# The two rings of matmul outputs in a mixture-of-experts stage, each cut to a depth of one

## The reference, cut to what matters

```python
x = x + _L0_gnn_ref(xn, edge_index, ...) + _L0_mix_ref(xn[None], ...)[0]
x = x + _L0_ffn_ref(_layernorm(x)[None], ...)[0]
# in _L0_ffn_ref:
#   a softmax over the edges that end in a node weighs the rows of its neighbours -> scores
topk_s, topk_i = jax.lax.top_k(scores, 2); w = softmax(topk_s)
for ei in range(4):
    g = jnp.where(topk_i == ei, w, 0.0).sum(-1)
    hh = jax.nn.gelu(x @ W1[ei] + b1[ei])            # 256 -> 512
    out = out + g[..., None] * (hh @ W2[ei] + b2[ei])  # 512 -> 256
```

## Time and profile before

| | us |
|---|---|
| median of 3 runs | 5559.33 |
| the profiled execution, its own time | 5560.58 |
| its span | 5558.8 |
| PE busy | 3511.5 (63%) |
| PE weight loads busy | 2291.2 (41%) |
| DVE busy | 2083.0 (37%) |
| ACT busy | 802.4 (14%) |
| POOL busy | 2839.8 (51%) |
| TensorE clock granted, mean | 0.801 of full |

### The profile page before, as it was taken

The page is one execution under the profiler, slowest core; times in us unless marked ns, Lnnn a source line. Parts: engine busy times, 40 slices in busy tenths (PEclk is TensorE's granted clock), DMA queues, the critical chain, the costliest instruction groups (busy, mean ns, idle before and its releaser), DMA issues. The chain is left out here.

```text
span 5558.8 us, 46231 instructions
## 1 busy us (share of the span) xinstructions
PE 3511.5 (63%) x12937; PEld 2291.2 (41%) x12938; DVE 2083.0 (37%) x4892; ACT 802.4 (14%) x1970; POOL 2839.8 (51%) x2937
## 2 busy tenths in 40 slices
PE   0688888888577767777242766666666666669300
PEld 0455555555455545555121443434343434346200
DVE  5455566565566555444010111112011111103278
ACT  4111111111011111111010101111111111112000
POOL 2666666666666666666657144444445353530420
PEclk6898999899788888888675888788877878789755
DMA  7444444444455555655121111111111111111297
GB/s 254 116 112 111 114 113 113 110 112 111 112 133 148 148 145 149 166 152 151 20 62 19 32 46 35 42 39 43 38 42 46 35 46 36 46 31 63 87 255 257
DMA packets 381413, 540.56 MB, mean 97 GB/s; under 512 B 120315, under 2 KB 297819, under 8 KB 381144
## 3 DMA queue, kind: packets, MB, share of 16 engines
q0 software_dynamic: 119136, 234.44, 19.2%
q1 hardware_dynamic: 243119, 288.12, 16.2%
q10 hardware_dynamic: 19016, 16.48, 0.9%
HBM read 392.03 MB, written 146.74 MB: 97 GB/s over the span
## 5 line engine op out<-in xcount | busy, mean ns | idle before, releaser
L787 POOL DMA_INDIRECT rows<-xn_rows,gsrc x1664 | 1611.5, 968 | 902.0 <-issue 458.8
L1353 POOL DMA_INDIRECT nb<-route_rows,idx x1024 | 1001.5, 978 | 1087.4 <-DVE msg L1428 772.7
L1092 PE MATMUL PS<-rows,oh 128*128 128x257 f32 x3328 | 908.3, 426 | 339.9 <-issue 215.3
L1682 PE MATMUL PS<-arena,hid 128*125 128x256 f32 x3200 | 773.2, 400 | 524.3 <-ACT hid L1643 311.5
L1674 PE MATMUL PS<-x2g,arena 128*128 128x500 f32 x1600 | 759.4, 634 | 314.8 <-issue 154.5
L1682 PEld LDWEIGHTS PS<-arena,hid 128*125 128x125 f32 x3200 | 633.5, 199 | 680.5 <-issue 577.6
L1092 PEld LDWEIGHTS PS<-rows,oh 128*128 128x128 f32 x3328 | 693.4, 214 | 470.9 <-issue 284.3
L1617 DVE TENSOR_TENSOR y_sb<-PS,b_b 125x512 f32<-125x512 f32 x200 | 128.7, 686 | 2010.5 <-PE PS L1682 1466.4
L1674 PEld LDWEIGHTS PS<-x2g,arena 128*128 128x128 f32 x1600 | 321.2, 204 | 732.1 <-issue 540.1
L1643 ACT ACTIVATE hid<-PS,b_sb 128x500 f32<-128x500 f32 x400 | 270.2, 678 | 1551.1 <-PE PS L1674 762.5
L1164 PE MATMUL PS<-own_w,p_t 128*125 128x512 f32 x400 | 228.8, 656 | 77.6 <-ACT s_t L1052 45.4
(11 more groups left out here) (304 smaller groups left out, 3088.6 us busy)
## 6 DMA issues: line engine op xcount, KB each, us to landing
y_rows<-y_sb SPq DMA_DIRECT2D x100, 512.0 KB
arena<-y_rows SPq DMA_DIRECT2D x100, 512.0 KB
rows<-xn_rows,gsrc POOLq DMA_INDIRECT x1664
nb<-route_rows,idx POOLq DMA_INDIRECT x1024
sum_rows<-kept SPq DMA_DIRECT2D x104, 128.5 KB
x_rows<-x SPq DMA_DIRECT2D x100, 128.0 KB
hid<-x_rows SPq DMA_DIRECT2D x100, 128.0 KB
m_in<-sum_rows SPq DMA_DIRECT2D x100, 125.5 KB
```

The lines of the kernel that those rows point to most:

```text
L787: pool.indirect_dma_start(out=rows[w][h][:, q, 0:D], out_offset=None, in_=xn_rows, in_offset=bass.IndirectOffsetOnAxis(ap=gsrc[:, s * HU + ...
L1092: last = mm(SUM[:, 0:D + 1], oh[w][h][:, q, :], rows[w][h][:, q, :], start=h == 0 and q == 0, stop=h == 1 and q == HU - 1)
L1353: pool.indirect_dma_start(out=nb[b % NBUF][:, c, :], out_offset=None, in_=route_rows, in_offset=bass.IndirectOffsetOnAxis(ap=idx[:, b * W ...
L1682: last = mm(Y[j % 2][e // 2][0:NP, (e % 2) * D:(e % 2 + 1) * D], hid[:, 4 * e + k, j * NP:(j + 1) * NP], w2_sb[:, e, k, :], start=k == 0, ...
```

## The change

Two expressions in PE's `group` are changed, and nothing else. Product c now waits until the Gelu of product c-1 is done, and tile j until the eviction of tile j-1 is done. The banks written, the instructions and their order stay as they are; in group 0, where the values are constants, three waits in the first half and one in the second that were left out are now there.

```diff
@@ -1669,14 +1669,14 @@
                     for c in range(16):
                         e = c // 4
-                        wait_after(pe, s_hid, g * 16 + (c - 3))
+                        wait_after(pe, s_hid, g * 16 + c)
                         for k in range(2):
...
                     pe.wait_ge(s_hid, g * 16 + 16)
                     for j in range(4):
-                        wait_after(pe, s_yc, g * 4 + (j - 1))
+                        wait_after(pe, s_yc, g * 4 + j)
                         for e in range(NE):
```

## The result

The changed kernel takes 5963.06 us (median of 4 runs, 5948.25 to 5968.37) against 5562.46 for the kernel before beside it (4 runs): 401 us slower, ratio 1.0716, 95% interval 1.0699 to 1.0734. The forecast was 5998, and slower. The profiled execution of the changed kernel is its fastest, 5948.25 us with a span of 5946.5; against the span of before that is 388 us more.

What follows compares the result with a forecast made beforehand. The experts' stage was taken as some 1120 us starved during POOL's fetches and 1230 us of PE at full pace. Terms 224, 150, 48, 7 and 10 sum to 439 us more, giving 5998 us, range 5855 to 6290.

Steps and rivals of the forecast that it cites:

- The product's wait: Experts' products on PE: each but a group's first costs 1.03 us more, period 1.68 to 2.71, 15.5 us a group.
- The tile's wait: Experts' tiles on PE: tiles 1 to 3 each cost 1.64 us more, 4.9 us a group.
- the DVE term: Evictions late behind DVE's scores and records: 0.5 us a batch and a few us for long scans, 10 in all.
- The groups without fetches: 11 of the experts' 25 groups, PE at full pace: each grows by 20.4 us, from 55.5 to 75.9; 224 in all.
- What starvation hides: During POOL's runs of fetches PE and ACT are slow (starved), which was to hide part of the new waits.
- The ten groups: Groups whose fetches fall on the products: some 14 us more each plus one tile gap, 15 against 20.4 unhidden; 150 in all.
- the three: Groups whose fetches fall on the end of the products and the tiles: 16 us more each, 48 in all.
- The clock: Rival: PE's clock falls in the cut stream, 1.76 us a product; 6236 us for half the products, 6470 for all; chance 0.22.
- The rival that starvation hides all of the products' wait: Stores on PE and ACT last longer, so the 13 groups with fetches lose only tile gaps: 5864 us; chance 0.11.
- The rival of no change: POOL's fetches pace the experts' stage, so each wait fills time PE loses anyway: time stays 5560 us; chance 0.03.
- The estimate that ACT's eight entries hold four Gelus: ACT's queue, two entries a Gelu, stores four Gelus when starvation begins, hiding a few us a group.
- The 35 matmuls at once behind a wait: Starved tiles on PE: 35 matmuls with their loads run at once, 70 instructions, agreeing with a queue of 64.

Runs made afterwards that it cites:

- e1: The kernel before with only the products' half of the change (each product waits for the Gelu of the one ahead): 5756.27 us, ratio 1.0436.
- e2: The kernel before with only the tiles' half of the change (each tile waits for the eviction of the one ahead): 5616.64 us, ratio 1.0186.
- e7: The kernel before with 60 of each batch's 64 fetches left out, missing rows read as zeros: 4603.33 us.
- e8: The changed kernel, both waits, with 60 of each batch's 64 fetches left out, missing rows read as zeros: 5128.55 us.
- e9: The changed kernel with each Gelu made twice and a drain between, to lengthen PE's rest between products: 6157.28 us.
- e4: The kernel before with ACT's own wait for s_y made once a group, not before each Gelu: 5509.93 us, ratio 0.9989.
- e3: The kernel before with product c waiting for the Gelu of product c-2, tiles as before: 5521.41 us, ratio 1.0008.
- e5: The kernel before with all batches of fetches hung on the second tile of a group: 5510.46 us, ratio 0.9913.
- e10: The kernel before with all batches of fetches but the last hung on the third tile of a group: 5560.34 us, ratio 1.0.
- e11: The kernel before with the change's tile wait, and products waiting for the Gelu of product c-2: 5691.3 us, ratio 1.0238.

## Why the prediction was right

The mechanism held: PE's two streams break at the waits, and each break costs what the rows of before said.

*The product's wait* was put at 1.03 us: measured 2.71 us from start to start against 1.68, with 0.77 us idle, to the last digit. e1 has it alone: 71.1 us a group, 15.5 more.

*The tile's wait* was put at 1.64: measured 8.55 against 6.91, idle 1.38. Where DVE's `records` comes before the next eviction the gap is 1.66, so the DVE term was 0.3 us a batch, not 0.5. e2's groups are 5.2 us longer, and the whole group of the change 20.7 where 20.4 stood.

*The groups without fetches* so cost 228 us (the eleven differences added up, the odd groups with them) against 224.

*What starvation hides* was the step without a row, and it is where most of the error lies. The ten groups cost 113 in place of 150, the three 39 in place of 48, and group 0 13 in place of 7: together 165 where 205 stood, 40 of the sum's 46 us too many. The other 6 are the term for DVE. The way in which time is lost held: 90 us behind the first fetch 10 to 12 Gelus were done, I had said 11, and the rest came in cycles of 4.4 and 2.7 us. But the last Gelu of the ten groups lies 12 us later behind the first fetch, where I had said 14. Some 2 us more a group are the clock, which I left out. Before, the tiles began at half clock after a rest, and the group's four tiles took 30.0 us on average instead of 27.7 (as in the second row, 30.36). In the changed kernel the clock comes back in the serial products at the end of starvation, and the tiles take 32.8, only 2.8 more and not 4.9. Group 5, first the start of its tiles before, then two stretches of the last products of the changed kernel:

```profile
3475.00:3478.00 3.00, 2.71 (x6) 2.15 (x7) 0.00 (x0) 1.44 (x2) 0.00 (x0) 0.50 0.00 0
```

```profile
3562.00:3566.00 4.00, 3.60 (x4) 1.06 (x4) 0.00 (x0) 0.37 (x1) 0.00 (x0) 0.50 0.01 2
3571.00:3575.00 4.00, 3.23 (x8) 1.10 (x7) 0.00 (x0) 0.68 (x1) 0.00 (x0) 1.00 0.00 0
```

So the prediction's sentence that after a rest the clock comes back only within an unbroken stream was wrong: here it came back between products with 0.77 us of rest before each.

The costs of the four kinds add up to 393 us, where the sum had 439, and the spans differ by 388. The medians differ by 401, since the profiled execution of the changed kernel is its fastest; that the forecast lies only 35 us off is luck in this part. e7 and e8 show the hidden part as a whole: 124 us, where the prediction had 71 (510 less 439).

*The rivals.* The clock did not fall, in groups without fetches it is 1.00 (0.99 and 0.95 in the last two), and in e9 it holds with PE at 56%. What the Trainium skill describes in "TensorE: Matmul & The Clock Gate", section "A second HAM failure mode: psum-queue depth-cycling", for a bf16 kernel was not seen in these fp32 products, at two lengths of rest (0.77 and 1.51 us). The rival that starvation hides all of the products' wait falls with the table: on top of the tiles' wait the products' one costs the ten groups 9.4 us (124.8 less 115.4). Its reason is seen in part: in e1, where the products come 2.71 us apart, ACT keeps that pace until 25 us or more behind the first fetch, where before it kept its pace until about 20. The measured 393 lies between this rival's 305 and my 439. The rival of no change falls with POOL's wait, which grew by 300 us; I had said 400 for that, and forgot that fetches start only from group 2 on and end at group 20, so that group 0 and the last four don't count.

*The queues.* The estimate that ACT's eight entries hold four Gelus, which I worked out from the Trainium skill's "TensorE: Matmul & The Clock Gate", section "Architectural detail", isn't borne out by e4: with one of the two waits a Gelu taken out fewer than two more Gelus ran at full pace on average, not four, and e3 had one more with both waits in place. The 35 matmuls at once behind a wait came back in e5 and (36) in e10.

## What to carry to other kernels

What a wait costs between two engines can be read in the trace of before, wherever the same hand-over already happens once: idle time, plus the overlap of neighbouring matmuls, plus the weight load that is no longer hidden. Here a ring's second bank paid for all of it (e3, ratio 1.0008); the third and fourth showed only beside the tiles' wait, in the groups where starvation makes one engine run late and the other ahead (118.5 us in e11 against 115.4 in e2). A kernel that alternates between a full-pace state and a starved one should be summed state by state, and a delay that falls into the starved state costs what the backlog costs at its end.

## What the runs showed of the hardware that I had not expected

Some 20 us after POOL begins a run of indirect DMAs of 128 rows, about 1.3 us apart, ACT's Gelus come 11.2 us apart and PE's pairs of weight load and matmul on the tiles 2.8, until about 8 us after the last. With 4 of 64 fetches a batch it is gone and the kernel takes 4603 us instead of 5560 (part of the work left out). What inside the chip causes it was not tried and stays open; e4 shows only that one wait a Gelu less on ACT doesn't change its pace. The cost of such a run depends on where it begins: 53.2 us beyond the 55.6 of a free group on the second tile (e5), 57.9 on the first (the ten groups of before).
